# Context stores waited out behind the query projection, and unread transposes where TensorE would stand

## The reference, cut to what matters

```
x = x + L0_xattn(_layernorm(x), ctx)   # self attention a1, then cross attention a2, each with an MLP
x = x + L0_attn(_layernorm(x))         # 16 heads, rotary
x = x + L0_ffn(_layernorm(x))          # routed experts
x = x + L1_xattn(_layernorm(x), ctx)   # one head
x = x + L1_attn(_layernorm(x))         # a recurrence over time
x = x + L1_ffn(_layernorm(x))          # routed experts with a capacity
x = x + L2_xattn(_layernorm(x), ctx)   # 16 heads of 64
x = x + L2_attn(_layernorm(x))
x = x + L2_ffn(_layernorm(x))
x = x + L3_xattn(_layernorm(x), ctx)   # 16 heads
x = x + L3_attn(_layernorm(x))
x = x + L3_ffn(_layernorm(x))
```

```
xn = _ln(x, lnx_g, lnx_b);  yn = _ln(y, lny_g, lny_b)      # y is the context, 8 x 1601 x 128
q = einsum('bsc,hcd->bhsd', xn, wq)
k = einsum('btc,hcd->bhtd', yn, wk);  v = einsum('btc,hcd->bhtd', yn, wv)
a = softmax(einsum('bhsd,bhtd->bhst', q, k) * D ** (-0.5))
o = einsum('bhst,bhtd->bhsd', a, v)
```

## Time and profile before

| | us |
|---|---|
| median of 3 runs | 2292.37 (2290.57 to 2295.74) |
| the profiled execution | 2297.82, of which its span is 2296.0 |
| PE busy | 2042.5 |
| DVE busy | 1379.2 |
| ACT busy | 1124.4 |
| POOL busy | 512.6 |

### The profile page before, as it was taken

One profiled execution on the slowest core, in us unless ns is written; L12 is line 12 of the kernel. 1 busy time (PEld: TensorE's weight loads), 2 busy tenths in 40 slices (PEclk: granted clock), 3 DMA queues, 4 the chain that ended last, 5 costly groups with the idle time before them and its releaser, 6 DMA issues. The chain is left out here.

```text
span 2296.0 us, 41893 instructions
## 1 busy us (share of the span) xinstructions
PE 2042.5 (89%) x14948; PEld 1749.3 (76%) x14948; DVE 1379.2 (60%) x2704; ACT 1124.4 (49%) x2256; POOL 512.6 (22%) x412
## 2 busy tenths in 40 slices
PE   4776999999886998489899999987979999999898
PEld 1654999999655885277699999956859999997577
DVE  6463777777445443831677777724447777776366
ACT  2243666666423432321566666613436666664254
POOL 2323222221011330200322222002332222220034
PEclk9687999999987998789999999977999999999799
DMA  5153010010041213432100100001221001000022
GB/s 211 25 233 128 31 45 31 29 44 0 26 156 57 79 53 136 188 139 83 45 30 31 45 29 29 0 13 66 78 83 45 31 30 44 29 15 0 19 78 76
DMA packets 32314, 144.01 MB, mean 63 GB/s; under 512 B 3632, under 2 KB 9136, under 8 KB 28848
## 3 DMA queue, kind: packets, MB, share of 16 engines
q1 hardware_dynamic: 32176, 142.23, 17.2%
HBM read 125.59 MB, written 13.90 MB: 61 GB/s over the span
## 5 line engine op out<-in xcount | busy, mean ns | idle before, releaser
L1037 ACT ACTIVATE pTh<-ps 128x512 fp32r<-128x512 f32 (+1 forms) x768 | 353.9, 519 | 382.5 <-PE ps L937 380.4
L1095 DVE TENSOR_TENSOR pTl<-ps,pTh 128x512 fp32r<-128x512 f32 (+1 forms) x768 | 415.7, 582 | 129.0 <-ACT pTh L1037 128.8
L637 PE MATMUL ps<-pTh,ch 128*128 128x256 f32 (+1 forms) x1248 | 383.5, 307 | 2.3 <-DVE pTl L1095 2.2
L638 PE MATMUL ps<-pTl,ch 128*128 128x256 f32 (+1 forms) x1248 | 348.4, 279 | 0.0
L639 PE MATMUL ps<-pTh,cl 128*128 128x256 f32 (+1 forms) x1248 | 348.0, 279 | 0.0
L637 PE MATMUL ps<-cTh,qh 128*128 128x512 f32 (+2 forms) x768 | 276.9, 361 | 15.2 <-POOL ql L891 8.0
L639 PE MATMUL ps<-cTh,ql 128*128 128x512 f32 (+2 forms) x768 | 269.6, 351 | 0.0
L638 PE MATMUL ps<-cTl,qh 128*128 128x512 f32 (+2 forms) x768 | 268.8, 350 | 0.0
L1082 DVE TENSOR_REDUCE top<-ps 128x1 f32<-128x802 f32 x192 | 189.2, 986 | 110.7 <-PE ps L639 110.7
L637 PEld LDWEIGHTS ps<-pTh,ch 128*128 128x128 f32 (+1 forms) x1248 | 235.1, 188 | 15.8 <-DVE pTl L1095 12.1
L638 PEld LDWEIGHTS ps<-pTl,ch 128*128 128x128 f32 (+1 forms) x1248 | 235.7, 189 | 0.0
(11 more groups left out here) (351 smaller groups left out, 3585.9 us busy)
## 6 DMA issues: line engine op xcount, KB each, us to landing
w<-l1f_w_in SPq DMA_DIRECT2D x16, 1024.0 KB, 8.0
raw<-ctxT_in SPq DMA_DIRECT2D x16, 801.0 KB, 4.3
raw<-ctx_in SPq DMA_DIRECT2D x14, 832.0 KB, 4.4
wg<-l0f_guide_in SPq DMA_DIRECT2D x10, 704.0 KB, 5.1
z<-ctx_in SPq DMA_DIRECT2D x8, 832.0 KB, 12.9
z<-z SPq DMA_DIRECT2D x8, 832.0 KB, 10.6
keys<-ctx_in SPq DMA_DIRECT2D x8, 832.0 KB, 11.2
zT<-zT SPq DMA_DIRECT2D x8, 801.0 KB, 14.0
```

Source lines behind the costliest of these rows:

```text
L637: pe.matmul(out, high, moving_high, start=start, stop=False)
L638: pe.matmul(out, high, moving_low, start=False, stop=False)
L1037: nc.scalar.activation(pTh[0:w, PARTS[g][0]:PARTS[g][0] + n, slot, :], ps[0:w, turned_bank[slot][g], 0:n * P].rearrange("p (k r) -> p k r" ...
L1095: dve.tensor_tensor(pTl[0:w, at, slot, :], ps[0:w, turned_bank[slot][g], 0:n * P].rearrange("p (k r) -> p k r", r=P), pTh[0:w, at, slot, : ...
```

## The change

1. **Stores waited out later.** `turn` no longer waits for the stores at the end of its block. The query projection follows as a block of its own inside it, with the wait as SP's part (`sync=stored`). Its results go to the halves of `mid` and `xn`, since `q` has no room yet.
2. **Next weights fetched later.** `fetch_next("a2")` moves behind the fetches of the first keys.
3. **First rows split by ACT and DVE.** In a2 only, the keys' rows are split at the end of ACT's and DVE's lists (`rows_on_scalar`, `rows_on_vector`) of the one block that is left, POOL splits the turned half there. l2x and l3x stay as they were.
4. **One block for the first three norms.** `normalise` is gone; `rows_to_norms` takes over with no products and three norms, tile by tile. It waits for the weights of a1 only where it first needs them (`landed`). All statistics of the context are made in the dense block behind it (`statistics`). ACT takes one square root of a constant in the program's first block.
5. **Places of the shares made early.** `inverse` and `heads` are made on POOL ahead of the queries (`share_places`), so that `late_values` has no POOL part.
6. **Transposes that nobody reads.** `turn_unused` makes `count` transposes of the identity. In `rows_to_norms` 5 stand ahead of each tile turned after the products, 8 at the end; in `self_attention` 18 stand after the first scores, 7 ahead of the last `turn_out` and 8 after it. In all there are 386: 30 times 5, 17 times 8, 4 times 18 and 4 times 7.

```diff
+            @block.scalar
+            def _(act):
+                act.wait_ge(filled, 4)
+                nc.scalar.activation(std[:, 0:1], eps[:], ACT.Sqrt, bias=zero[:])
...
-        def normalise(src, z, turned=(), add=(), affine=None, dve_aside=None):
...
+        def turn_unused(pe, bank, count):
+
+            for n in range(count):
+                pe.transpose(ps[:, bank, 0:P], ident[:], ident[:])
...
-        def rows_to_norms(products, norms, turned, pool=None):
+        def rows_to_norms(products, norms, turned, pool=None, landed=None):
...
-                    for t in range(NT - per - 1, NT):
+                    for t in range(max(NT - per - 1, 0) if products else 0, NT):
+                        turn_unused(pe, 7, 5)
                         turn_tile(pe, t, norms[-1][1], 4 + t, z_ready, turned_ready)
+                    turn_unused(pe, 0, 8)
...
+                        if step == per + 1 and landed is not None:
+                            landed(act)
...
+                        if step == 2 and landed is not None:
+                            landed(dve)
...
                         scores(0)
+                        turn_unused(pe, 4, 18)
                         for t in range(NT):
...
                             values(t)
+                        pe.wait_ge(exp_ready, 2 * NT)
+                        turn_unused(pe, 4, 7)
                         turn_out(NT - 1)
+                        turn_unused(pe, 4, 8)
...
+                    def rows_on_scalar(act):
+                        act.wait_ge(keys_landed, 16)
+                        nc.scalar.activation(ch[:, 0], first_keys[:], ACT.Copy).then_inc(rows_high, 1)
+
+                    def rows_on_vector(dve):
+                        dve.wait_ge(rows_high, 1)
+                        dve.tensor_tensor(cl[:, 0], first_keys[:], ch[:, 0].bitcast(F32), ALU.subtract).then_inc(first_low, 1)
...
+        def share_places(dh, where):
+
+            sums = sb("sums", [P, B * H], where=where)
+            inverse = sb("inverse", [P, B, 32], where=where)
+            heads = sb("heads", [2 * 32, H * dh], F32R, where)
+            nc.gpsimd.memset(inverse[:], 0.0)
+            pick = ident[0:2 * 32, 0:2 * 32].rearrange("p (e j) -> p j e", e=2)[:, 0:H // 2, :]
+            nc.gpsimd.tensor_copy(heads[:].rearrange("p (j e d) -> p j e d", e=2, d=dh),
+                                  pick.unsqueeze(3).broadcast_to([2 * 32, H // 2, 2, dh]))
...
-                        dve.wait_ge(cleared, 1)
                         dve.tensor_tensor(total, halves[:, :, :, 0], halves[:, :, :, 1], ALU.add).then_inc(added, 1)
...
-            weights_here("a1")
...
-                    normalise(x, xn)
-                    normalise(xn, inner, affine=(w("ln1_g"), w("ln1_b")))
-                    normalise(inner, xn, [(xT, w("lnx_g"), w("lnx_b")), (yT, w("lny_g"), w("lny_b"))],
-                              dve_aside=context_z.first_statistics)
+                    rows_to_norms([], [(x, xn, (), None), (xn, inner, (), (w("ln1_g"), w("ln1_b"))), (inner, xn, (), None)],
+                                  [(xT, w("lnx_g"), w("lnx_b")), (yT, w("lny_g"), w("lny_b"))],
+                                  landed=lambda engine: weights_landed(engine, "a1"))
+                    weights_here("a1")
...
-                fetch_next("a2")
                 w = a2
-                context_z.turn(w("lny_g"), w("lny_b"))
+                flat_mid, flat_xn = (t.rearrange("p t d -> p (t d)") for t in (mid[:], xn))
+                qT = [t[:, n * N:(n + 1) * N] for t in (flat_mid, flat_xn) for n in range(2)]
+                context_z.turn(w("lny_g"), w("lny_b"),
+                               lambda stored: dense(feature_rows(w.chunks("wq", KC), xT, qT), sync=stored))
...
+            def project(with_first, with_second, rows_on_scalar, rows_on_vector):
+                fetch_next(fetched)
+                if qT is not None:
+                    dense(head_queries(w.chunks("wkT", per), qT, q, dh), pool=with_first, act_end=rows_on_scalar,
+                          dve_end=rows_on_vector)
+                    return
...
+                    def all_stored(sp):
+                        sp.wait_ge(z_stored, 16 * B)
+                        sp.wait_ge(zT_stored, 16 * B)
...
-                            sp.wait_ge(z_stored, 16 * B)
-                            sp.wait_ge(zT_stored, 16 * B)
```

More of the change, by code:

```diff
@@ L93 @@
 RoutePlaces = namedtuple("RoutePlaces", "count small eight index where first second row pair")
+SharePlaces = namedtuple("SharePlaces", "sums inverse heads")
 ContextKeys = namedtuple("ContextKeys", "cTh cTl ch cl raw fetch_keysT fetch_keys")
-ContextNormaliser = namedtuple("ContextNormaliser", "fetch first_statistics other_statistics deviations first_rows second_rows "
+ContextNormaliser = namedtuple("ContextNormaliser", "fetch statistics deviations first_rows second_rows "
                                                     "vector_rows last_rows store_rows turn")
@@ L242, in dense @@
-        def dense(products, pool=None, dve=None, act=None, sync=None):
+        def dense(products, pool=None, dve=None, act=None, sync=None, act_end=None, dve_end=None):
             def nth(n):
@@ L434, in either, with part @@
             return "act" if n % 2 else "dve"
+        def part(rows, m):
+            return rows[m] if isinstance(rows, list) else rows[:, m, :]
         def feature_rows(w, src, dst, column=None, chunks=None, engine=None):
@@ L1856, in two_attentions @@
             with ExitStack() as tmp:
                 q = sb("q", [P, H, N], where=tmp)
-                sums = sb("sums", [P, B * H], where=tmp)
-                with context_keys(dram["zT"], dram["z"], queries(w, 4, HP, q)) as context:
-                    cross_attention(q, HP ** -0.5, context, sums, gain=w("lny_g"))
+                places = share_places(HP, tmp)
+                with context_keys(dram["zT"], dram["z"], queries(w, 4, HP, q, "a2", qT)) as context:
+                    cross_attention(q, HP ** -0.5, context, places.sums, gain=w("lny_g"))
@@ L1982, in store_rows, with turn, turn_block @@
                         store_row(sp, b)
-                def turn(gamma, beta):
-                    with ExitStack() as late, nc.Block() as block:
+                def turn(gamma, beta, meanwhile):
+                    def all_stored(sp):
+                        sp.wait_ge(z_stored, 16 * B)
+                        sp.wait_ge(zT_stored, 16 * B)
+                    with ExitStack() as late:
                         zT = sb("zT", [P, B, KEVEN], where=late)
+                        turn_block(zT, gamma, beta)
+                        meanwhile(all_stored)
+                def turn_block(zT, gamma, beta):
+                    with nc.Block() as block:
                         def cols(g):
@@ L2076, in many_head_cross @@
                 q = sb("q", [P, H, N], where=tmp)
-                sums = sb("sums", [P, B * H], where=tmp)
+                places = share_places(dh, tmp)
                 with context_keys(dram["ctxT"], dram["ctx"], queries(w, per, dh, q, name)) as context:
-                    cross_attention(q, scale, context, sums)
+                    cross_attention(q, scale, context, places.sums)
                 oT = sb("oT", [P, per, N], where=tmp)
```

120 lines of the change are left out of this document (31 added, 89 removed).

## The result

The changed kernel takes 2267.68 us (median; 2265.85 to 2281.63) beside 2293.73 us for the kernel before (2290.57 to 2296.59, on the same chip): a ratio of 0.9902, with a 95% interval of 0.9877 to 0.9927. That is 26 us less. Its profiled execution took 2266.19 us (span 2264.4, mean clock 0.955), 31.6 us less than that of before. The forecast was 2262 us, in a range of 2246 to 2280.

What follows compares the result with a forecast made beforehand. TensorE, busy 89% of the span, was taken as the bound, so gains were sought where it stands. 4.0 + 9.6 + 2.1 + 8 + 6 = 29.7 us off a median of 2292.4 gave 2262 us, range 2246 to 2280.

Steps and rivals of the forecast that it cites:

- Part 1: Start of the program: DVE norms once x lands, TensorE starts at 28.2 instead of 32.63, scores of a1 4.0 us sooner.
- Part 2: Context stores and a2's query projection: stores end earlier, projection hidden in the wait, first cross scores sooner; 9.6 us gain.
- starting as POOL's ends: Sign of a right forecast: in a2's split of the key rows, DVE's subtraction begins when POOL's subtraction ends.
- only bytes decide: At the context's turn, bytes alone set when the stores end; moving 2.23 MB of weights behind them saves 5.7 us.
- rival (c): At the context's turn, the stores end no earlier or the rows land late: 5.7 us less gain, 2268 us; chance 0.11.
- part 4: Unread transposes raise the clock: 8 us net gain in the four self attentions, 6 us net in norm stages.
- 0.11 of clock is 3.3 us: Self attentions l2a and l3a: same 552 matmuls, 24.1 us at 0.76, 27.4 at 0.65; or 3 us for 0.1.
- rival (b): Unread transposes bring as much as they cost, the clock falling elsewhere: 15.7 us gain remain, 2276 us; chance 0.18.
- part 3: Late values: without POOL's clearing there, DVE's addition ends sooner, 1.2 us at l2x and 0.9 at a2, together 2.1.
- rival (a): At l2x's late values the shorter gap keeps the clock up: 13 us more gain, 2250 us; chance 0.15.
- Rival (d): Slower: unread transposes don't hold the clock, and TensorE comes last to every block's end; +16 us, 2308; chance 0.04.

## Why the prediction came out

**Right, by its steps.** Part 1: first product forecast at 28.2 and measured at 28.60, scores of a1 at 58.1 and 58.56. Part 2: 9.6 forecast, 10.6 measured, 38.55 us from the turn to the scores against 39.5. Inside, the weights were worth 7.1 to 7.3 us, not 5.7, and the way from the stores' end to the scores won 3.3 us, not 3.9 (the key fetch landed 5.5 us behind its issue, where 4.4 was taken). DVE's subtraction ran 1.75 us behind the end of POOL's, forecast 2.2. As recorded it began 1.53 us before that end, and the sign "starting as POOL's ends" was met only by its end. The projection was over before the stores were, so it was hidden. So the argument "only bytes decide" held, and rival (c) fell. One slip in part 1 did no harm: DVE's own chain is 36.0 - 6.3 = 29.7 us, not 29.4, and the 57.8 goes by the former.

**Wrong: the size of part 4.** 14 us were forecast, and the runs with and without differ by 3.2 us in the median and by nothing in the ratio. The step that failed is "0.11 of clock is 3.3 us": it was read from two attentions that did the same work, and applied to attentions with 33 more matmuls. The grant rose by more than was forecast in three of the four, and by 0.06 in a1. By the prediction's rate of 3 us for 0.1 these rises (0.06, 0.17, 0.24 and 0.16) are 18.9 us, and the four stretches got 2.7 us shorter. Where nothing else spoils it, in l2a, 0.24 of clock went with 3.0 us and not 7. So the price was set too low (4 to 6 us for the four), or the rate too high; the runs don't part the two. The term also has no line for what was seen next in some of the stretches: the gap in TensorE's own instructions, and in l0a the wait for `v`, with the low clock behind each. This is the outcome of rival (b), "because the clock falls in other places instead", at 0.18.

**Wrong in the profiled pair: the size of part 3 at l2x.** 1.2 us forecast, 9.6 in the profiled pair. The length of the gap and DVE's addition came out as written (over with POOL's bias, 1.12 us of wait left), but the clock behind it was taken as given. That was rival (a), at 0.15, and its argument against ("TensorE was busy for 21.43 of those 23.1 us, and the clock still did not rise") shows that a clock once low stayed low there, and says nothing on whether it falls. Over unprofiled runs the move alone is worth 3.2 us (0.2 to 6.2): that takes in the forecast's 2.1 for both places and leaves out the 13 of rival (a). So the 9.6 us belong to this pair of profiles, and the term's size over many executions was about right.

In the profiled pair both happened at once and cancelled, +8.4 at l2x (9.6 for 1.2) against -6.9 in attentions and the rest (7.1 for 14). So 2268 for the profiled execution was met (2266.19) from a sum of which two terms are wrong, and that is luck; parts 1 and 2, 13.6 forecast and 14.2 measured, are not.

Rival (d) has its answer too. The turn of the context is 104 transposes and nothing else, and the grant went from 0.50 to 1.00 within it before; in the kernel after the same 104 take 11.18 us in place of 13.46, at 1.00 from their start. The Trainium skill's rule ("TensorE: Matmul & The Clock Gate", "Part 4: PE-mode transpose") that the full clock doesn't engage for transposes does not hold for these, which are fp32.

**Wrong: from the profile to the median.** 5.4 us were taken off because the profiled execution of before lay that far above its median. Its second profile lay there too (2298.3), while the changed kernel's first lay 1.5 us below its own median and its second 11.9 us above it. One profiled execution says little on the median of this kernel. The gain by medians is 26.0 us, 3.7 less than the sum, and that is the distance between 2262 and 2268, together with 1.4 us by which the median of before had moved (2293.73 for 2292.37), and rounding.

**Open.** Which of the differences between unprofiled executions (2265.85 to 2281.63 for one program) are such falls could not be seen, since only the profiled ones have a clock record by stretch. Why the unread transposes in norm stages lose 9 us alone and nothing beside the others is open too: the loss stands in the self attentions, most of it in l2a, which has two gaps in its scores in that profile (0.53 and 0.57 us). And parts 1 to 3 by these experiments, 14.2 us and 3.2 us, leave 8.6 of the 26.0 us, of which part 4 has between nothing and 3.2. The intervals are some 6 us wide to either side, so no owner can be named for the rest.

## What to carry to other kernels

Work that only keeps TensorE's clock up has a price in TensorE's own time: multiply its count by its duration at both clock levels before the gain is believed, and compare the length of the stretch, not its grant. Where a gap of a few us stands ahead of a long stretch of small matmuls, shorten the gap by moving another engine's work out of the way: that gave 3.2 us here (0.2 to 6.2), and the 386 transposes gave nothing that can be told from zero. Before a stage is sped up at its start, look for the next transfer that it will then wait for. A wait for a store that is bound by bytes can be filled with work that needs none of them, with the next big load behind it in the queue.

## What the hardware showed that was not expected

- TensorE can stand in the middle of independent matmuls. At the full clock 64 of the scores take 0.91 us, and gaps marked "issue" of 0.2 to 2.1 us appear within them, after 44 and after 33 of the 64 in both executions of the changed kernel in l3a, and at other places in other kernels. In the stretch around the one in l3a of the kernel after, from 2128 to 2134, the only DMA traffic is two packets of the kind "instruction", of 0.02 and 0.01 MB. That they are its cause was not tested; in the run with twice as many unread transposes the gap did not appear.
- The clock behind a gap is not fixed by the gap's length: a 2.34 us gap at l2x was followed by 0.52 in the kernel before, and by 1.00 where the same gap was put back into the changed kernel. One program gave 24.0 and 31.2 us for l0a in two executions, the longer one with the clock high at its start and a wait of 2.33 us for a load. The kernel before repeated its falls in both of its executions.
- One and the same DVE addition of 64 numbers a partition took 0.23 us with POOL at rest, 1.02 us beside POOL's making of `heads` and 2.41 us beside its bias of 2.35 us.
